# Halved bulk transfers, eight slots for gathered rows and fewer semaphores in the last stage of a two-layer graph network

## The reference

```python
# layer 0: attention over the edges of a destination, 8 heads of 16
Q = (x[src] @ Wq + bq); K = (x[dst] @ Wk + bk); Vv = (x[dst] @ Wv + bv)
scores = (Q * K).sum(per head) / 4 + edge_attr_64 @ Wb + bb
ex = exp(scores - segment_max(scores, dst)[dst])
alpha = ex / segment_sum(ex, dst)[dst]
x1 = layernorm(x + segment_sum(alpha * Vv, dst) @ Wo + bo)     # all 50,000 rows
# layer 1: one softmax over all edges
h = x1 @ W
e = leaky_relu((h @ a[:128])[src] + (h @ a[128:])[dst], 0.2)
out = layernorm(x1 + segment_sum(softmax(e)[:, None] * h[src], dst))
```

## Time and profile before

| | us |
|---|---|
| runs before | 1257.95, 1265.93, 1266.73 |
| median | 1265.93 |
| the profiled execution | 1259.13 |
| its span | 1257.4 |
| first stage, from PE's first step to POOL's last gather | 50 to 594 |
| second stage, POOL's gathers | 640 to 940 |
| last stage, POOL's scatters | 954 to 1255 |

### The profile page before, as it was taken

One profiled execution on the slowest core, in us unless ns is written; L12 is line 12 of the kernel. 1 busy time (PEld: TensorE's weight loads), 2 busy tenths in 40 slices (PEclk: granted clock), 3 DMA queues, 4 the chain that ended last, 5 costly groups with the idle time before them and its releaser, 6 DMA issues.

```text
span 1257.4 us, 14313 instructions
## 1 busy us (share of the span) xinstructions
PE 718.7 (57%) x3271; PEld 482.5 (38%) x3271; DVE 759.0 (60%) x3537; ACT 717.2 (57%) x2048; POOL 764.1 (61%) x807
## 2 busy tenths in 40 slices
PE   0357767767667767676844564546455554544441
PEld 0235445445445544444634454545442211111110
DVE  4487767767777668677756555546437444444442
ACT  3457777777777777777713343424347554444443
POOL 7665666666666666665056665666654666666666
PEclk9888888787887888878967777767767766777775
DMA  7365565566665656654155767667755333433331
GB/s 211 110 187 158 184 209 168 178 188 214 203 200 200 203 161 193 197 166 163 68 171 162 216 207 221 198 211 223 208 172 163 121 113 115 119 116 120 107 107 46
DMA packets 89104, 209.87 MB, mean 167 GB/s; under 512 B 20602, under 2 KB 22793, under 8 KB 89008
## 3 DMA queue, kind: packets, MB, share of 16 engines
q1 hardware_dynamic: 63802, 161.20, 40.4%
q0 software_dynamic: 25216, 47.76, 13.6%
HBM read 122.85 MB, written 90.07 MB: 169 GB/s over the span
## 4 chain that ended last, share of the span: by engine, by line
another core or an unknown queue 19%; DVE 17%; ACT 13%; issue 8%; PE 5%; POOL 1%; DMA 1%; DVEq 0%; SPq 0%; POOLq 0%
ACT yb L801 3%; ACT node_out L801 2%; ACT src_b L952 2%; PE psum L748 2%; DVE src_b L1477 2%; DVE match L1152 2%; ACT xsT L961 2%; DVE nst L1492 1%; DVE nst L1254 1%; POOL out_dram L524 1%; DMA x1d_in<-x_all 1%; DVE shift L1485 1%; ACT h_res L965 1%; DVE node_in L1247 1%
## 5 line engine op out<-in xcount | busy, mean ns | idle before, releaser
L518 POOL DMA_INDIRECT xs<-in_x,src_tab x196 | 185.7, 947 | 153.0 <-remote 74.6
L524 POOL DMA_INDIRECT out_dram<-yb,at_last x196 | 194.7, 993 | 120.7 <-ACT yb L801 64.6
L518 POOL DMA_INDIRECT xs<-x_all,row_tab x196 | 187.5, 957 | 114.9 <-issue 55.8
L518 POOL DMA_INDIRECT h_res<-in_x,dst_tab x196 | 188.9, 964 | 59.8 <-issue 59.8
L801 ACT ACTIVATE h_res<-node_in,shift,rstd 128x128 f32<-128x128 f32 (+1 forms) x392 | 155.8, 482 | 0.3 <-DVE shift L1284 0.3
L776 PE MATMUL psum<-src_b,ident_inv 128*128 128x512 f32 x90 | 69.6, 865 | 132.8 <-DVE src_b L1477 111.7
L961 ACT ACTIVATE xsT<-psum 128x512 f32<-128x512 f32 x48 | 28.7, 597 | 200.0 <-remote 165.8
L606 PE MATMUL psum<-h_res 128*128 128x512 f32 x98 | 68.7, 789 | 120.9 <-ACT h_res L808 120.0
L748 PE MATMUL psum<-w,xsT 128*128 128x129 f32 x384 | 80.7, 376 | 91.8 <-ACT xsT L961 80.4
L748 PEld LDWEIGHTS psum<-w,xsT 128*128 128x128 f32 x384 | 71.6, 278 | 99.1 <-ACT xsT L961 86.6
L610 PE MATMUL psum<-xsT,h_res 128*128 128x512 f32 x98 | 85.2, 966 | 32.2 <-ACT xsT L812 19.4
(11 more groups left out here) (312 smaller groups left out, 1915.5 us busy)
## 6 DMA issues: line engine op xcount, KB each, us to landing
x1d_in<-x_all SPq DMA_DIRECT2D x98, 256.0 KB
node_in<-in_x SPq DMA_DIRECT2D x48, 512.0 KB
x_all<-h_res SPq DMA_DIRECT2D x48, 512.0 KB
out_dram<-node_out SPq DMA_DIRECT2D x48, 512.0 KB
x_all<-yb SPq DMA_DIRECT2D x49, 256.0 KB
src_b<-src_t SPq DMA_DIRECT2D x49, 256.0 KB
agg_rows<-src_b SPq DMA_DIRECT2D x49, 256.0 KB
node_in<-x_all SPq DMA_DIRECT2D x24, 512.0 KB
```

The lines of the kernel that those rows point to most:

```text
L518: return pool.indirect_dma_start(out=to, out_offset=None, in_=table, in_offset=bass.IndirectOffsetOnAxis(ap=idx, axis=0))
L524: return pool.indirect_dma_start(out=table, out_offset=bass.IndirectOffsetOnAxis(ap=idx, axis=0), in_=rows, in_offset=None, bounds_check=l ...
```

## The change

Bulk transfers of node chunks (in, x1 out, result out, and the late ones of the second stage) are issued as two halves of 256 KB, by columns. The semaphores of gathered tiles now stand for pairs of tiles (head and rest), and SP's steps wait for the pairs of a group before they issue: in the first stage for those of group s, in the second for those of the x1 rows of group s. The stores of the result move ahead of the loads in SP's step, one half in each of two steps. In the second stage the gathered rows have eight slots, four of xs and the four of yb, so POOL waits for x1_T of g - 8. Waits for the stored x1 chunks stand before the late loads and before POOL's first gather of x1. In the last stage the chain of running sums and the moments are ordered by drains of the engine's own pipe in place of waits on its own semaphores: r_chain and xa_done are posted once for a group, e_stats and e_log are gone, and DVE's running sums and moments are interleaved.

```diff
--- before.py
+++ after.py
+    XG = XS + YB
+    PAIR = G // 2
...
+    SPREAD = GROUPS - 7
...
+        def summed(g):
+            return G + g
...
+        def x1_rows(g):
+            u = g % XG
+            return xs[:, u, :] if u < XS else yb[:, u - XS, :]
+
+        def x1_landed(g):
+            u = g % XG
+            halves = (src_head, src_rest) if u < XS else (dst_head, dst_rest)
+            in_first_stage = len(range(u % XS, GROUPS, XS))
+            return [half[u % XS] for half in halves], 16 * PAIR * (in_first_stage + use(g, XG))
...
+        def nodes_landed(eng):
+            for k in range(GROUPS - NX, GROUPS):
+                eng.wait_ge(x1_stored[k % NX], landed(k, NX))
...
-            def move_nodes(to, of, k, done):
-
+            def move_nodes(to, of, k, done, half):
+                cols = slice(half * BW // 2, (half + 1) * BW // 2)
                 for lo, hi in spans(k):
-                    sp.dma_start(to[lo:hi, :], of[lo:hi, :]).then_inc(done, 16)
-
-            def load_nodes(k):
+                    sp.dma_start(to[lo:hi, cols], of[lo:hi, cols]).then_inc(done, 16)
+
+            def load_nodes(k, halves=(0, 1)):
                 wait(sp, x1_applied, k - NI + 1)
-                move_nodes(node_in[0:parts(k), k % NI, :], node_chunk(x, k), k, node_loaded[k % NI])
+                for half in halves:
+                    move_nodes(node_in[0:parts(k), k % NI, :], node_chunk(x, k), k, node_loaded[k % NI], half)
...
+            def store_out(k, halves=(0, 1)):
+                o = out_no(k)
+                if k >= 4:
+                    sp.wait_ge(y_applied, k - 3)
+                else:
+                    sp.wait_ge(x1_applied, k + 3)
...
+            def pair_here(halves, g):
+                sp.wait_ge(halves[g % XS], 16 * PAIR * use(g, XS))
...
-                g = s - 4
-                if edge(g):
-                    if g == END:
-                        sp.wait_ge(last_applied, 2)
-                    else:
-                        sp.wait_ge(y_applied, g + 1)
-                    sp.dma_start(edge_group(x1d_rows, g), yb[:, g % YB, :]).then_inc(x1d_stored[g % YB], 16)
-                k = s + AHEAD - 1
-                if 2 <= k < GROUPS:
-                    load_nodes(k)
-                k = END if s == END + 1 else s + AHEAD - 4
-                if edge(k) and (k < END or s == END + 1):
-                    sp.wait_ge(x1_applied, k + 1)
-                    move_nodes(node_chunk(x1_all, k), node_x1[0:parts(k), k % NX, :], k, x1_stored[k % NX])
-                k = s + AHEAD - 6
-                if edge(k) and not late(k):
-                    o = out_no(k)
-                    move_nodes(node_chunk(out, k), node_out[0:parts(k), o % NO, :], k, out_stored[o % NO])
-                if s >= 0 and s % EB == EB - 4 and s // EB + 1 < GROUPS // EB:
+                if 1 <= s <= SPREAD:
+                    pair_here(src_head, s)
+                    if edge(s - 5):
+                        store_rows(s - 5)
+                    if edge(s - 2) and not late(s - 2):
+                        store_out(s - 2, (1,))
+                    if not late(s - 1):
+                        store_out(s - 1, (0,))
...
+                if 1 <= s <= SPREAD:
+                    pair_here(src_rest, s)
+                    load_nodes(s + 4, (0,))
+                    pair_here(dst_head, s)
+                    load_nodes(s + 4, (1,))
+                    store_x1(s + 1, (0,))
+                    pair_here(dst_rest, s)
+                    store_x1(s + 1, (1,))
...
+                    nodes_landed(sp)
...
+            def pair_landed(g, half):
+                if g < END:
+                    halves, value = x1_landed(g)
+                    sp.wait_ge(halves[half], value)
+
+            for r in range(SB, SB + 3):
+                load_more(r)
+            for s in range(GROUPS + 2):
                 j = s // 2 - 1
-                if s % 2 == 0 and 0 <= j < len(LATE):
-                    sp.wait_ge(late_applied, 2 * (j + 1))
-                    sp.dma_start(node_chunk(out, LATE[j]), node_out[:, j % NO, :]).then_inc(late_stored[j % NO], 16)
-                    if j + NI < len(LATE):
-                        load_late(j + NI)
+                for half in (0, 1):
+                    if edge(s):
+                        pair_landed(s, half)
+                    if half == 0:
+                        load_more(s + SB + 3)
+                    elif s >= 2 and edge(s + 2):
+                        sp.wait_ge(dots_done, s + 2 - XI + 1)
+                        load_x1d(sp, s + 2, x1d_got)
+                    if 0 <= j < len(LATE):
+                        if s % 2 == 0:
+                            store_late(j, half)
+                        elif j + NI < len(LATE):
+                            load_late(j + NI, (half,))
...
+            nodes_landed(pool)
             pool.wait_ge(fix_stored, 16)
             for g in range(GROUPS):
                 pool.wait_ge(row_done, g + 1)
-                wait(pool, x1_T, g - XS + 1)
+                wait(pool, x1_T, g - XG + 1)
                 for t, idx in enumerate(columns(row_tab, g)):
-                    gather(tile(xs[:, g % XS, :], t), x1_all, idx)\
-                        .then_inc(last_x1 if g == END and t == G - 1 else got_x1[g % XS], 16)
+                    gather(tile(x1_rows(g), t), x1_all, idx)\
+                        .then_inc(last_x1 if g == END and t == G - 1 else x1_landed(g)[0][t // PAIR], 16)
...
-                wait(act, r_chain, (g - 1) * G)
+                if g >= 2:
+                    act.wait_ge(r_chain, summed(g - 2))
                 for t in tiles:
                     i = g * G + t
-                    fn(tile(xa[:, g % 2, :], t), h_res[:, i * DH:i * DH + D], ACT.Copy, scale=att[:, i:i + 1])\
-                        .then_inc(xa_done, 1)
+                    last = fn(tile(xa[:, g % 2, :], t), h_res[:, i * DH:i * DH + D], ACT.Copy, scale=att[:, i:i + 1])
+                    if g == 0:
+                        last.then_inc(xa_done, 1)
+                if g > 0 and tiles.stop == G:
+                    last.then_inc(xa_done, 1)
...
-                fn(logs[:, 0:G], nmv[:, s % 2, :, 1], ACT.Ln, bias=eps_cols[:, 0:1]).then_inc(e_log, 1)
-                act.wait_ge(e_log, s)
+                fn(logs[:, 0:G], nmv[:, s % 2, :, 1], ACT.Ln, bias=eps_cols[:, 0:1])
+                act.drain()
...
-                dve.wait_ge(xa_done, g * G + (t if g == 0 else G - 1) + 1)
-                wait(dve, r_chain, g * G + t)
+                if g == 0:
+                    dve.wait_ge(xa_done, t + 1)
+                    wait(dve, r_chain, t)
+                else:
+                    if t == 0:
+                        dve.wait_ge(xa_done, summed(g))
+                    dve.drain()
                 if t == 0 and g >= NA:
                     dve.wait_ge(agg_stored[g % NA], use(g - NA, NA) * 16)
                     wait(dve, e_y, g - NA)
                 prev = tile(agg[:, g % NA, :], t - 1) if t else tile(agg[:, (g - 1) % NA, :], G - 1)
-                v.scalar_tensor_tensor(tile(agg[:, g % NA, :], t), prev, same_prev[:, g * G + t:g * G + t + 1],
-                                       tile(xa[:, g % 2, :], t), ALU.mult, ALU.add).then_inc(r_chain, 1)
-
...
-            def moments(b):
-                dve.wait_ge(e_y, b)
-                wait(dve, e_var, b - 1)
-                for t in range(G):
-                    last = v.bn_stats(nst[:, t, :], tile(bank[b % 4], t))
-                last.then_inc(e_stats, 1)
+                add = v.scalar_tensor_tensor(tile(agg[:, g % NA, :], t), prev, same_prev[:, g * G + t:g * G + t + 1],
+                                             tile(xa[:, g % 2, :], t), ALU.mult, ALU.add)
+                if g == 0 or t == G - 1:
+                    add.then_inc(r_chain, 1)
+
+            def moments(b, t):
+                v.bn_stats(nst[:, t, :], tile(bank[b % 4], t))
 
             def aggregates(b):
-                dve.wait_ge(e_stats, b)
                 if b == 2:
                     dve.wait_ge(first_shift_done, G)
-                wait(dve, e_shift, b - 2)
                 wait(dve, e_rstd, b - 2)
+                dve.drain()
                 for t in range(G):
                     last = v.bn_aggr(nmv[:, b % 2, t, :], nst[:, t, :])
                 last.then_inc(e_var, 1)
...
-                    for t in range(1, G):
-                        running(s, t)
+                    running(s, 1)
                 if edge(s - 1):
-                    moments(s - 1)
+                    dve.wait_ge(e_y, s - 1)
+                    moments(s - 1, 0)
+                    if edge(s):
+                        running(s, 2)
+                    moments(s - 1, 1)
+                    if edge(s):
+                        running(s, 3)
+                    moments(s - 1, 2)
+                    moments(s - 1, 3)
                     aggregates(s - 1)
```

118 lines of the change are left out of this document (79 added, 39 removed).

## The result

Beside each other on one chip the kernel before took 1263.51 us (median of 4) and the changed one 1300.07 (median of 4, 1284.97 to 1308.50); the ratio is 1.0269, with a 95% interval of 1.0213 to 1.0325. I had forecast 1228, with 1180 to 1272 as the range. The profiled execution of the changed kernel is its longest, 1308.50 us with a span of 1306.8, and the ratio leaves it out as a slow run. The four differences between stages that follow add up to 49 us, where the ratio makes 34 (1.0269 of 1263.5) and the medians 37: some 12 to 15 us of them are this execution's own.

The account below looks back on a forecast made before the run. It took POOL's issuing and the end of the hold on PE's posts as the bound. 1259.13 + 0 + 2 - 5 - 30 = 1226 us against the profiled execution, stated as 1228 us, range 1180 to 1272.

Parts of the forecast that it names:

- The first stage, 0 us: First stage: no change, as POOL's list and waits stay and PE's added waits end inside a hold of 3.07 us.
- met already: First stage: SP's new waits come late enough to cost nothing, the gathers having landed 17 us earlier.
- Second stage, -5 us: Second stage: eight slots lengthen POOL's first burst by two groups and save two of 24 pauses of 2.39 us.
- bounded it at +43: Second stage, upper bound: bursts of two groups that all start 1.8 us later would cost 43 us.
- Last stage, -30 us: Last stage: shorter late steps give POOL bursts of about 12 groups, 5.54 us a group in place of 6.14.
- A held step: Last stage: a late step loses waits of 1.22 and 4.44 us and takes 8.6 us in place of 17.
- The first rival: Last stage: drains bring nothing, as the hold falls on what is left; 1256, or 1248 to 1264; chance 0.19.
- Between the stages, +2 us: Between first and second stage: SP's wait for the last x1 chunk costs 2 us, the middle of 0 and 4.4.
- My third rival: Whole kernel: the hold on posts goes away and POOL is the bound throughout; 1160 or 1090; chance 0.11.
- the rival of 1276 to 1291: Second stage: POOL's bursts start on row_done, stay two groups long, +1.03 us a group, +48 us; chance 0.12.

Follow-up runs that it names:

- slots_alone: The kernel before with eight slots for the gathered x1 rows and nothing else of the change; 1285.03 us against 1259.18, ratio 1.0216.
- four_slots: The changed kernel with four slots for the x1 rows in place of eight, all else kept; 1268.36 us, ratio 1.0071 to the kernel before.
- drains_alone: The kernel before with only the change's last stage (drains, fewer posts, interleaving); 1263.92 us against 1259.18, ratio 1.0035.

## Why the prediction was wrong

**The first stage, 0 us: wrong by its cover.** The step is 12.0 us as I had said (353.38 to 365.40), with PE's post as the last thing awaited. But SP's pair waits are not "met already" everywhere: together with the halves they go with 4 to 10 us on late chips. I worked out one step in the middle from the rows and left out the start of the loop and its irregular steps. The profiled execution is 11 us behind at group 8 (112.7 against 101.5), of which some 5 can be chance. The halves did not load the DMA engines more: they are busy for 0.58 x 562 = 326 us, and were for 0.60 x 544 = 326.

**Second stage, -5 us: the step that failed.** It is +25 us (slots_alone +26, the changed kernel against four_slots +25). The step is the one by which I chose between the bounds, "the first burst is longer by two groups for certain and saves two of the 24 pauses". I had bounded it at +43, had the mechanism as a rival with its place and price (POOL starts on row_done, a held post and 2.2 us of DVE later, bursts of two groups), and gave it 0.12. The first burst is longer, six groups in place of four, and next to nothing follows from it, while the later start comes with every burst: the 21 bursts after it are all two groups long, with pauses of 3.3 us on average (70.2 us in 21), where the kernel before has 2.5 (59.1 in 24). Of the 25 us, 16.5 lie in POOL's gathers (314.8 us against 298.3) and 9 between its last gather and its first scatter; in slots_alone it is 24 and 2. Forty-nine groups at 26 us is 0.53 us a group and not the rival's 1.03, as it had put the pause at 4.25 us (1.75 + 2.2 + 0.3). (L1160's row ends at 725.71, not 725.78 as I read it; nothing hangs on that.) The gain and the loss were both worked out in the text, and the sum took the small, certain one.

**Last stage, -30 us: the step that failed by most.** The step is "A held step is then about 4.6 + 3.3 + 0.7 (logarithm, exponential, shift) = 8.6 us in place of 17": it takes the waits of 1.22 and 4.44 us away and puts a drain at 0. The held step was 14.2 us, not 17, and is 14.1 with the drains. These stand still just as the waits did, 1.56, 1.56, 1.64 and 3.44 us in the step above, and ACT waits 9.32 us where it waited 10.12. In the three late steps shown the end comes 1.5 to 2.9 us after POOL's burst, with waits or drains in them. The first rival came nearest ("a drain waits for the held post itself", 0.19), though the drains have no post to wait for. The sum had a slip too: a step of 8.6 us against POOL's 5.16 takes 0.67 group off the lead, not 0.4, so a burst would be about 8 groups and the gain some 20 us by its own rule. The stage is +1.5 us in the changed kernel and +3.5 in drains_alone.

**Between the stages, +2 us:** 49.5 us where it was 47.5. The size is as said; it was the middle between two bounds, so in part luck, and no run tests its cause.

**What I didn't see** is that the hold is not on every chip. My third rival, that it might go away, gave 1160 and 1090; on a chip without it the kernel before takes 1041, with nothing changed. The measured time lies above the range because I had given the rival of 1276 to 1291 only 0.12 (with its own terms, 1259 + 2 + 48 - 30, the lower of the two is 1279) and ended the range at 1272.

The sum that the runs give: 25 us for the slots, 4 for the drains, 4 to 10 for pair waits and halves, 33 to 39 us where the ratio makes 34 and the medians 37.

## What to carry to other kernels

A wait that lasts until another engine stops is not bridged by giving that engine more slots, nor was it shortened here by fewer posts: look first at what ends it (here, in the steps shown of all three stages, that POOL had issued its last transfer 1.5 to 3 us earlier), then try a short pause in the engine that goes with it. More slots change which semaphore is the last to be met; before adding them, follow what the new one hangs on, and move that ahead by as much. And time a change on more than one chip before its tenths of a per cent are believed: here a change of 2.7% on one is 0.1% on another.

## What the runs showed of the hardware

- Chips, or their states at the time, differ by more than any change here. With the same kernel, four late chips took 1252 to 1261 us and two prompt ones 1041 and 1042. Single instructions take as long on both (a gather 0.96 us, a scatter 0.99 us of issuing); what differs is when posts arrive. The mean granted clock was 0.76 to 0.80 on the late ones and 0.82 to 0.85 on the prompt ones, but for a run at 0.67 on a late chip and one at 0.55 on a prompt chip (1102.76 us); the engines stand idle more on the first, so this may follow from the waits. The run at 0.67 took 1261.21 us, no longer than others there, so the clock is not what makes a chip late. Why a chip is late stays open.
- On a late chip, while POOL issues indirect transfers back to back, posts between PE, DVE and ACT come late, in the rows shown a single one by up to 4.6 us (DVE's e_var to ACT), and a step with several of them takes 14 us in place of 3.3. In the last stage this begins some 11 us after POOL went on (POOL at 1078.91, DVE idle from 1090.13, in the kernel before). Some posts get through while POOL issues; in the steps shown the last one does so 1.5 to 3 us after POOL's last transfer.
- Drains of DVE are held too, with no post in them: 1.56 to 3.44 us each in a late period (1120.31 to 1128.75 of the changed kernel). In an undisturbed step five of them and the interleaving take 0.12 to 0.22 us together.
- A fill on POOL lets posts through as idling does. POOL had no wait for ACT before its next pause after five of five fills of 2.70 us, and after two of five idle pauses of 1.5 us; after fills of 2.26 us none followed in six of eleven cases.
